# Attention output projection: a third unit's upper four heads as three fp32r products

## The reference, cut to what matters

```python
h1 = adaln(x, t, norm1_w, norm1_b)          # layernorm(x)*(1+scale)+shift
x = mha(h1, h1, ...) + x                    # attention 1: 16 heads of 64
h2 = adaln(x, t, norm2_w, norm2_b)
x = mha(h2, context, ...) + x               # attention 2: 16 heads of 64
h3 = adaln(x, t, norm3_w, norm3_b)
x = glu_ff(h3, w1, b1, w2, b2) + x          # x@w1 -> a*gelu(gate) -> @w2
...
logits = router(layernorm(x))               # outer products, softmax, weighted sum over 8 experts
top_k(logits, 2) -> scores                  # then two experts of 352 hidden units per token
```

## Time and profile before

| | |
|---|---|
| median of three runs | 2181.36 us |
| profiled execution | 2183.79 us, its span 2181.9 us |
| granted PE clock, mean over the span | 0.987 |
| PE busy | 2061.1 us (94%), 11132 instructions |
| ACT busy | 1403.8 us (64%) |
| DVE busy | 1325.6 us (61%) |
| POOL busy | 1083.2 us (50%) |

### The profile page before, as it was taken

The page is one execution under the profiler, slowest core; times in us unless marked ns, Lnnn a source line. Parts: engine busy times, 40 slices in busy tenths (PEclk is TensorE's granted clock), DMA queues, the critical chain, the costliest instruction groups (busy, mean ns, idle before and its releaser), DMA issues. The chain is left out here.

```text
span 2181.9 us, 38680 instructions
## 1 busy us (share of the span) xinstructions
PE 2061.1 (94%) x11132; PEld 1351.1 (62%) x11132; DVE 1325.6 (61%) x3405; ACT 1403.8 (64%) x2665; POOL 1083.2 (50%) x1214
## 2 busy tenths in 40 slices
PE   6899999999999999999999999999999787898896
PEld 5455565555665555555656565565655466788895
DVE  4554657676766666666666666767654744455465
ACT  4566666676767676767676767676766566565563
POOL 1443443636373736373736454554544463546653
PEclk9999999999999999999999999999999899999998
DMA  4111111111111112111111111211114121112266
GB/s 131 48 35 29 49 34 49 45 54 44 48 44 51 57 38 58 44 48 53 39 53 43 48 53 40 61 44 48 39 35 124 45 59 35 55 49 61 60 187 201
DMA packets 134529, 127.36 MB, mean 58 GB/s; under 512 B 14665, under 2 KB 108521, under 8 KB 134442
## 3 DMA queue, kind: packets, MB, share of 16 engines
q1 hardware_dynamic: 125162, 108.03, 17.8%
q0 software_dynamic: 9280, 18.28, 2.5%
HBM read 86.63 MB, written 40.67 MB: 58 GB/s over the span
## 5 line engine op out<-in xcount | busy, mean ns | idle before, releaser
L1844 POOL TENSOR_TENSOR pr<-pr,sm 128x512 f32<-128x512 f32 x256 | 277.7, 1099 | 482.7 <-DVE sm L1397 482.7
L1073 ACT ACTIVATE kp<-ps 128x512 f32<-128x512 f32 x512 | 298.9, 601 | 181.7 <-PE ps L281 175.1
L799 PE MATMUL ps<-tt,V 128*128 128x512 f32 x768 | 381.1, 594 | 3.5 <-ACT tt L1073 3.5
L1387 DVE TENSOR_REDUCE mx<-ps 128x8 f32<-128x512 f32 x256 | 176.8, 690 | 309.1 <-PE ps L748 309.1
L1073 ACT ACTIVATE tt<-ps 128x512 f32<-128x512 f32 x512 | 275.3, 591 | 40.0 <-PE ps L778 39.9
L748 PE MATMUL ps<-kp,hf 128*64 128x256 f32 x2048 | 279.2, 395 | 12.9 <-DVE pr L1390 9.6
L281 PE MATMUL ps<-cT,M 128*128 128x512 f32 x768 | 261.7, 464 | 0.0
L748 PEld LDWEIGHTS ps<-kp,hf 128*64 128x64 f32 x2048 | 125.5, 137 | 203.5 <-DVE pr L1390 140.2
L281 PE MATMUL ps<-hk,M 128*128 128x512 f32 x768 | 244.7, 442 | 1.9 <-DVE hk L1451 1.9
L1073 ACT ACTIVATE pt<-ps 128x512 f32<-128x512 f32 x256 | 153.6, 600 | 142.9 <-PE ps L760 139.9
L900 PE MATMUL ps<-xT,wt 128*128 128x128 f32 (+1 forms) x1728 | 224.1, 281 | 18.0 <-DVE ux L1657 7.3
(11 more groups left out here) (229 smaller groups left out, 3599.0 us busy)
## 6 DMA issues: line engine op xcount, KB each, us to landing
mod<-emb_s SPq DMA_DIRECT2D x96, 256.0 KB, 4.3
xr<-rows_s SPq DMA_DIRECT2D x144, 66.0 KB
cb<-y_s SPq DMA_DIRECT2D x32, 256.0 KB
x_in<-in_x_dram SPq DMA_DIRECT2D x16, 256.0 KB, 4.4
xn_s<-x_in SPq DMA_DIRECT2D x16, 256.0 KB, 2.0
res<-xn_s SPq DMA_DIRECT2D x16, 256.0 KB, 2.8
c_in<-in_ctx_dram SPq DMA_DIRECT2D x16, 256.0 KB, 4.7
y_s<-res SPq DMA_DIRECT2D x16, 256.0 KB, 2.0
```

The costliest lines, as they stand in the source:

```text
L799: mm = nc.tensor.matmul(psO[:], Vw[a][:, g * HG + head_at(h), :], tt[:, h, :], start=(g == 0 and h == 0), stop=ends)
L1073: return nc.scalar.activation(o, i, ACT.Copy)
L1387: nc.vector.tensor_reduce(mx[:, p % 2, :], heads(psS[p % 2][:]), AX_X, ALU.max).then_inc(max_done, 1)
L1844: tensor(v, v, sm[:, p, :].unsqueeze(2).broadcast_to([P, HG, 64]), ALU.mult).then_inc(prob_done, 1)
```

## The change

Unit 1 joins the units whose upper four heads are projected as three fp32r products, so slot 2 now also hosts POOL's six split instructions, ACT's `last_split` and DVE's `last_rest`. In that slot `last_rest` stands at h = 3, behind `ln_lo(c, 2)` and ahead of `ln1`; `router_dot` goes from ahead of `ln1` (h = 4) to behind it (h = 5). POOL's `router_mul` moves from h = 2 to h = 1; since `prob` is now issued one tile ahead there, it still stands between `prob` of tile 2 and `prob` of tile 3. The weight matrices of unit 1 are held like those of unit 0; the total of SBUF is the same. The counting of splits goes from two to three per round.

```diff
-            M0, V0 = sa("M0", [P, 2, H, D], F32R), sa("V0", [P, H, D])
+            M0, V0 = sa("M0", [P, 2, H, D], F32R), sa("V0", [P, 2, HF, D])
-            RU = (3, 0)
-            R0 = sa("R0", [P, 2, HR, D], F32R)
+            RU = (3, 0, 1)
+            R0, R1 = (sa(f"R{u}", [P, 2, HR, D], F32R) for u in range(2))
-            Mw, Vw, Vr = [M0, M1], [V0, V1], {0: R0, 3: R3}
+            Mw, Vw, Vr = [M0, M1], [V0, V1], {0: R0, 1: R1, 3: R3}
@@ split_seq
-                return 0
+                return u
-                return 2 * NC - 1
-            return 2 * i - (u == 0)
+                return 3 * NC - 1
+            return 3 * i - 1 + u if u < 2 else 3 * i + 1
@@
+        def whole(u):
+            return V0[:, u] if u < 2 else V1[:, (u - 2) * HG:(u - 1) * HG]
@@ project
-                    mm = nc.tensor.matmul(psO[:], Vw[a][:, g * HG + head_at(h), :], tt[:, h, :], start=(g == 0 and h == 0), stop=ends)
+                    mm = nc.tensor.matmul(psO[:], whole(u)[:, h if u in RU else head_at(h), :], tt[:, h, :], start=(g == 0 and h == 0), stop=ends)
@@ ACT, setup
-                        copy(Vw[a][:, 8 * (g // 2) + g % 2:8 * (g // 2) + 8:4, :], src[:, :, 0, :])
+                        copy(whole(unit)[:, at:at + 2, :], src[:, :, 0, :])
@@ DVE, hooks of slot 2
-                         2: ((2, 3, router_sum), (4, 3, router_dot), (3, 2, lambda c: ln_lo(c, 2)), (4, -1, ln1), (6, 2, lambda c: glu_mul(c, 0)), (7, 2, lambda c: glu_split_lo(c, 0)), (8, -1, lambda c: ln_lo(c, 0)), (8, 3, top_first)),
+                         2: ((2, 3, router_sum), (3, 2, lambda c: ln_lo(c, 2)), (4, -1, ln1), (5, 3, router_dot), (6, 2, lambda c: glu_mul(c, 0)), (7, 2, lambda c: glu_split_lo(c, 0)), (8, -1, lambda c: ln_lo(c, 0)), (8, 3, top_first)),
@@ DVE, slot
-                    if h == 2 and last and lu in RU:
+                    if h == (3 if u == 2 else 2) and last and lu in RU:
                         last_rest(li, lu)
@@ POOL, hooks of slot 2
-                         2: ((2, 3, router_mul), (4, 3, router_out)),
+                         2: ((1, 3, router_mul), (4, 3, router_out)),
```

## The result

The kernel after takes 2197.06 us (median of four runs, 2194.27 to 2200.65) against 2180.8 for the kernel before (2178.35 to 2181.72): ratio 1.0073, 95% interval 1.0055 to 1.009. It is slower by 16 us; the forecast was 13.3 us slower, 2194.7, from 2181.36. The profiled execution has a span of 2198.8 us, 16.9 more than before, at a mean granted clock of 0.985 (before 0.987).

What follows compares the result with a forecast made beforehand. PE, busy 99.91 of 100 us, was taken to set the pace. 12 x (-0.59 + 0.52 + 1.0) = 11.2, + 2.0 + 0.2 - 0.1 = +13.3 us on 2181.36 gave 2194.7 us; 8-in-10 range 2177 to 2202.

Steps and rivals of the forecast that it cites:

- PE's products: Slot 2, heads 4 to 7 and a key product: fp32r takes 3.54 instead of 4.13 us, saving 0.59 us a round.
- ACT's copy: Slot 2, last tile's copy delays the layernorm and PE's feed-forward product: wait 0.14 becomes 0.66, costing 0.52 us a round.
- DVE against POOL: Slot 2, rounds 3 to 14: POOL's queued work shuts out DVE's rest and `ln1`; PE stalls about 1.0 us a round.
- The sum: Slot 2, rounds 3 to 14: saving, copy and stall add to 12 x (-0.59 + 0.52 + 1.0) = 11.2 us.
- SP's loads: Store of the normalized chunk and next modulation load come 3.4 us later, with slot 3 (30.6 us) to spare; no cost.
- Round 0: Slot 2: `ln1` now stands behind the rest and POOL's splits, reaching PE at 96.3 instead of 93.74; net cost 2.0 us.
- B: Slot 2: ACT's copy costs 0.52 but `ln1` gets through in time; +1 us, 2182.5 us; chance 0.22.
- C: Slot 2: the copy's delay is hidden and `ln1` is in time; -7.4 us on average, 2174.0 us; chance 0.14.
- D: Slot 3: scores also wait for the chain from `ln1` to the last key copies; +21.7 us, 2203 us; chance 0.10.

Runs made afterwards that it cites:

- f3: The kernel after, but PE projects unit 1's upper four heads as one fp32 product, with splits, copies, waits and order kept; ratio 1.0089.
- e2: The kernel after, with POOL waiting in slot 2 for the end of `ln1` before `prob` of tiles 1 to 3 and `router_mul`; ratio 1.0042.
- f2: f1 without POOL's added wait for `ln1`; ratio 1.0022 to the kernel before.
- f1: The kernel after with e1, e2 and e3 together, `router_dot` behind `glu_mul` and its split, round 0's rest behind `ln1`; 2145.39 against 2153.25 us, ratio 0.996.
- e4: The kernel after with DVE's order of before in slot 2: rest at h = 2 ahead of the lower part, `router_dot` ahead of `ln1`; ratio 1.0082.
- e1: The kernel after, with ACT's copy of the last tile in slot 2 moved behind the layernorm's upper part, ahead of key copy 3; ratio 1.0049.
- e3: The kernel after, with SP's load of `c_tm` moved ahead of its wait for `ln1` and of the modulation loads; ratio 1.0045.

## Why the prediction was right, point by point

- *PE's products*: 0.59 us a round forecast, 0.56 to 0.58 measured in the kernel after, 0.63 between f3 and the kernel after. Right.
- *ACT's copy*: the start of the feed-forward product moved as forecast (to 15.89 us into the slot). The price was mis-sized, 0.32 us instead of 0.52. The prediction took the 0.14 us ahead of that product for a wait that PE loses in full, and added 0.52 to it; by the rows of round 2 and of the middle round the 0.14 cost nothing, and of 0.65 the first 0.4 or so is covered by the fp32 product in front. The sentence ahead of the prediction that the distance from one start to the next is what an instruction costs does not hold behind an fp32 product.
- *DVE against POOL*: right in place, mechanism and size. POOL's end, the length of the rest and the end of `ln1` came within 0.1 us. The stall was 1.09 us (forecast 0.9 to 1.1). e2 and f2 against f1 show the cause, since there only POOL's start is moved. The Trainium skill, "SBUF — State Buffer", section "Who interferes with whom", says that issue order decides who blocks; e4's row, where DVE came first and POOL's instruction took 1.64 us instead of 1.28, agrees. The expectation of e4 had let POOL go first there, and missed by that.
- *The sum* of a slot 2: -0.59 + 0.52 + 1.0 = +0.93 forecast, -0.58 + 0.32 + 1.09 = +0.83 measured (0.81 by the slots): 9.7 us in twelve rounds instead of 11.2. The two stalls are not independent, as e1 shows: PE goes on when `ln1` ends, and what the first stall takes less the second takes more. So the mis-sized ACT term hardly touched the sum of rounds 3 to 14; it was right because the end of `ln1` was (22.18 for 22.1 to 22.3). Where no `ln1` binds, the price of ACT's copy does count: round 2 gained 0.58 us and round 15 0.31, for 0.07 each in the forecast.
- *SP's loads*: this step failed. It named the store and the modulation load that wait for `ln1` and left out what is queued behind them. The load of `c_tm` was issued 4.6 us ahead of slot 3 before and 2.2 after; 2.3 us in all, which the sum had at nothing. e3 shows it.
- *Round 0*: the wait was right (96.61 for 96.3; 2.3 to 2.4 us net for 2.0), the cost was not: +3.7 instead of +2.0, since the granted clock was at its lower level behind the wait in this execution.
- *Rivals*: B and C are out. D did not happen in the kernel after; e2 produced something near it.

That the total came within some 3 us is in part luck. Against the 13.3 us forecast, rounds 3 to 14 gave 1.5 less in slot 2 and rounds 2 and 15 0.7 less, while SP's load gave 2.3 more and round 0 1.7 more, most of it the clock; neither the load nor the clock was in the forecast (14.7 us in the first five rows of the table, slots 0 and 1 included); 2.2 us more in the profiled execution are in rounds 16 and 17 and stay unexplained.

## What to carry to other kernels

When work is added to an engine that has time to spare, ask which instructions of the neighbour it will now overlap, and not only whether it is done in time: POOL's added work was never late for anyone, and cost DVE 2.7 us in each round at the one place where PE was waiting for DVE. A wait added on the idle engine can then be the cure (12.6 us here). And after a semaphore that comes later, walk every queue behind its waiters to the last DMA.

## What the runs showed of the hardware that I had not expected

- A DVE instruction over SBUF and a POOL instruction over SBUF alternate when both queues are full: per POOL instruction of 1.0 us, one of DVE's 0.25 us `tensor_scalar` went through (four took 3.01 us where three of them met POOL, 3.76 in e1 where all four did, against 1.02 alone). DVE's reductions over 512 elements and its additions with one input from PSUM keep their times beside POOL (0.63 to 0.68 and 0.69 us, beside it or not).
- An fp32 product of 512 columns takes 0.86 us, but the fp32r product behind it starts after 0.46, and the remaining 0.40 is in the time of what follows. A wait of 0.14 us at that place cost PE nothing, one of 0.40 (round 2 of the kernel after, 252.99 to 255.33 us) 0.08, and one of 0.65 cost 0.32.
